# A convolution layer with neighbourhood attention: both transposes of the probabilities in one place

## The chip, the core and the metric

The kernel runs on one core of a Trainium2 chip. The metric is the device time of one execution in microseconds (us). Its engines work side by side and meet only at semaphores: TensorE (matrix products, in the rows PE, its weight loads PEld, its queue PEldq), VectorE (DVE), ScalarE (ACT), GpSimd (POOL, idle here after the start) and SyncE (SP), which issues the transfers.

## The reference, cut to what matters

Eight images of 128 x 128 pixels and 64 channels in fp32.

```python
stk = neighborhood(x)                       # 3x3 shifted views of x, zero padded
scores = einsum('bhwke,bhwe->bhwk', stk @ K_P, x @ Q_P) * mask
alpha = softmax(scores)                     # over the 9 neighbours
t_in = t = x + einsum('bhwk,bhwke->bhwe', alpha, stk @ V_P)
t = relu(conv3x3(t, ff1) + b1)              #  64 ->  64 channels
t = relu(conv3x3(t, ff2) + b2)              #  64 -> 128 channels
t = relu(conv3x3(t, ff3) + b3)              # 128 ->  64 channels
return t_in + t
```

## The kernel before, in words

The images are worked in 4 pairs, the 64 channels of one image on partitions 0 to 63 and of the other on 64 to 127. An image is cut into 16 bands of 8 rows. A pair takes 16 steps: k = 1 to 15, and k = 0 in which the last rows of one pair and the first of the next are worked together. Step G works the attention of band b = G + 1, the scores and softmax of band b + 2, the first convolution, and with one band's delay the second and third one. The names `k`, `b` and `att` in the code are these; `att == ASK` are the 60 steps in which a band of probabilities is still wanted. 53 of them run in a loop, which TensorE's code has for k = 2 to 15; k = 1 and k = 0 stand outside it, since their tiles leave rows out.

The three 3x3 convolutions use a one-dimensional Winograd form along the width: pairs of neighbouring columns are turned into four streams (`transform`, VectorE), four products are formed per pair, and sums and differences give the two output columns (`middle`, `outer`). Tile j of a convolution is one of the four streams. First and third convolution are fp32 products; a fp32 product shows as two half products in the trace. The second is taken from a high and a low part: `duh` (ScalarE, `u_high`) and `dul` (VectorE, `u_low`), times `w2h` and `w2l`. Its work on TensorE is 36 rounds, in each of which a product on the lower 64 rows of the array and one on the upper 64 run side by side: per tile j `begin2` (4 rounds), `go_on2` (2) and `end2` (3).

The attention of a band works on 16 patches of 8 x 8 pixels with their 10 x 10 = 100 keys. For a band, TensorE forms `r_product` and, masked, the `scores` (L426, L434); VectorE takes the maxima (`max_scores`, L932), ScalarE the exponentials with their sums (`exps`, L774), VectorE scales them (`scale`, L939 the reciprocal, L943 the multiplication, which raises `prob_ready`); TensorE transposes them (`turn`, L443: 16 transposes of 64 x 100 for each half of the band's patches, which raise `turned`), ScalarE copies them to SBUF (`keep_turned`, L791, raises `probt_ready`), and a step later TensorE mixes the keys with them (`mix`, L455) and forms the `v_product` (L465), to which VectorE adds x (`add_x`, L954). Half 0 of the scores lies in `far_banks`, half 1 in `near_banks`; the transposes of a half go to the same banks.

Each engine runs a program of its own, written out by hand for a step, and there is no planner. The parts that matter here:

- TensorE, `step` (L695 on): r_product, first convolution, v_product and scores between its parts, tiles 0, 1, 2 of the third convolution (`conv3_tile`, L514), the mixes, tile 3, then the second convolution with one half transposed ahead of `begin2(0)` and the other inside `go_on2(0)`. The waits for the second scaling stand in a function that `conv3_tile` and `go_on2` call in their middle (`ahead`): tile 3 has six taps, and it calls `ahead` before the last two (L525).
- `await_turn(b, half)` (L648) waits for `y_ready` (half 0 only) and for `prob_ready` of the half.
- VectorE, `step` (L1111 on), from add_x to the end: add_x, the inputs of the third convolution, the middle sums of the first, maxima 0, `outer1`, maxima 1, more inputs, middle sums of the third convolution (L1001, L1002), `scale(b + 2, 0)`, `u_low` 0 (L987), `scale(b + 2, 1)`, `outer3` (L1039, which waits for tile 3), `u_low` 1, `finish`, the inputs of the first convolution of the next step, middle sums of the second (L1005, L1006).
- ScalarE, `step` (L891 on): `keep_y` twice, `u_high` 1, `keep_turned` 0 and 1, then the copies of the second convolution.
- SyncE copies the last rows of `dodd` and `deven` to their front once tile 3 is done (L374 to L376); the next step's inputs wait for it.
- `begin2(0)` waits for the readers of the third convolution's banks 0 and 1 and for `duh`; `begin2(1)` for outer3 (L551); `begin2(2)` for `probt_ready` of both halves, because it overwrites their banks (L554).

Of the kernel before, what the change touches and what calls it, by code (L numbers as in the profile page):

```python
# [52 lines left out]
def bank_of(which, j):  # L53
    return j if which == CONV3 else 2 * j + (which == EVEN)


V, MIX, ASK = 1, 2, 3
# [10 lines left out]
def pairs3(k):  # L68
    return (0, 2) if k == LAST else (0, RP)
# [11 lines left out]
def build(nc, x_bands, x_keys, qt2, kt, vbd, w1, w2, w3, b1, b2, b3, window, eye, eye16, out):  # L81
    with ExitStack() as ctx:
# [6 lines left out]
        def sem(name):  # L89
            return ctx.enter_context(nc.semaphore(name))  # L90
# [98 lines left out]
        prob_ready = sem("prob_ready")  # L189
# [3 lines left out]
        y_ready = sem("y_ready")  # L193
# [47 lines left out]
        def middle_read(G, which, behind=0, image=1):  # L241
            n = {CONV1: 1 + image, CONV3: 4, ODD: 6, EVEN: 7}[which]
            return G * DVE_READS + (n + DVE_READS - DVE_READS * behind - (3 if G is FINAL else 0))

        def outer_read(G, which, behind=0):
            n = {CONV1: 3, CONV3: 5, ODD: 8, EVEN: 9}[which]
            return G * DVE_READS + (n + DVE_READS - DVE_READS * behind - (3 if G is FINAL else 0))
# [7 lines left out]
        def parts(G, part, behind=0):  # L255
            return G * 2 + (part + 1 + 2 - 2 * behind)
# [146 lines left out]
        def _(pe):  # L403
# [36 lines left out]
            def turn(b, half):  # L440
                for a in range(HALF):
                    for n, rows in enumerate((LOWER, UPPER)):
                        last = nc.tensor.transpose(score_banks[half][0:KEYS, n, a * C:(a + 1) * C],  # L443
                                                   prob[rows, 2 * half + a // GROUP, a % GROUP], eye_sb[rows, rows])
                        if a == HALF - 1:
                            last.then_inc(turned, 1)
# [49 lines left out]
            def conv3_tile(G, k, j, ahead=None):  # L496
                if j == 0:
                    pe.wait_ge(dve_read, middle_read(RUN, EVEN) if G is FINAL else middle_read(G, CONV1, image=0))
                elif j == 1 and G is not FINAL:
                    pe.wait_ge(dve_read, middle_read(G, CONV1))  # L500
                elif j == 2 and G is not FINAL:
                    pe.wait_ge(dve_read, outer_read(G, CONV1))
                lo, hi = pairs3(k)
                m, part = STREAMS[j], j // 2
                bank = conv_banks[:, bank_of(CONV3, j)]

                def tap(odd, s, start, stop):

                    rows, source = (LOWER, UPPER)[odd], (dodd, deven)[s % 2]
                    spans = [(lo, hi)]  # L510
                    if k == 1 and s in (0, 3):
                        spans = [(0, 2), (3, RP)] if s == 0 else [(0, 1), (2, RP)]
                    for lo_, hi_ in spans:
                        mm = nc.tensor.matmul(bank[rows, lo_ * 128:hi_ * 128], w3f[:, m, s, odd * C:odd * C + C],  # L514
                                              source[:, lo_ + s // 2:hi_ + s // 2, m], start=start,
                                              stop=stop and hi_ == hi)
                    return mm

                pe.wait_ge(d_done[ODD], parts(G, part, 1))
                tap(0, 2, True, False)  # L520
                tap(1, 2, True, False)
                tap(0, 0, False, False)
                pe.wait_ge(d_done[EVEN], parts(G, part, 1))
                tap(1, 1, False, False)
                if ahead:  # L525
                    ahead()
                tap(0, 1, False, True)
                tap(1, 3, False, True).then_inc(tile_done, 1)

            def tap2(k, which, j, rows, s, w, d, start, stop):  # L530

                lo, hi = pairs2(k)
                spans = [(lo, hi)]
                if k == 0 and (which, rows) == (EVEN, LOWER) and s == 0:
                    spans = [(0, 1), (2, RP)]
                if k == 0 and (which, rows) == (ODD, UPPER) and s == 1:
                    spans = [(1, RP)]
                for lo, hi in spans:
                    mm = nc.tensor.matmul(conv2_bank(which, j)[:, lo * 128:hi * 128],  # L539
                                          w[rows, STREAMS[j], 2 * (which == EVEN) + s],  # L540
                                          d[rows, lo + s:hi + s, STREAMS[j]], start=start, stop=stop)
                return mm
# [22 lines left out]
            def go_on2(G, k, j, ahead=None):  # L565

                pe.wait_ge(du_low, G * 2 + (j // 2 + 1))
                for s in range(2):
                    if ahead and s == 1:
                        ahead()  # L570
                    even = tap2(k, EVEN, j, LOWER, s, w2h, dul, False, False)
                    odd = tap2(k, ODD, j, UPPER, s, w2h, dul, False, False)
                even.then_inc(half_done, 1)
                odd.then_inc(half_done, 1)
# [66 lines left out]
            def await_v(G, b, att):  # L641
                if att:
                    pe.wait_ge(dve_read, outer_read(G, EVEN, 1))
                    pe.wait_ge(y_ready, b * 2 + 2)
                if att == ASK:
                    pe.wait_ge(r_ready, b * 2 + 6)

            def await_turn(b, half):  # L648
                if half == 0:
                    pe.wait_ge(y_ready, b * 2 + 4)  # L650
                pe.wait_ge(prob_ready, b * 2 + (half + 5))

            def values_and_scores(b, att):
                if att:
# [40 lines left out]
            def step(G, k, b, att):  # L695
                if att == ASK:
                    r_product(b + 2)
                if k in (0, DRAIN):
                    wholes(k, False, True, lambda: await_v(G, b, att))
                    quarters(k, False, False)  # L700
                    values_and_scores(b, att)
                    wholes(k, True, True)
                    quarters(k, True, False)
                else:
                    quarters(k, False, True)
                    if att:
                        pe.wait_ge(dve_read, outer_read(G, ODD, 1))
                        pe.wait_ge(y_ready, b * 2 + 2)
                        pe.sem_inc(phase_begun)
                        v_product(b)  # L710
                    if att == ASK:
                        pe.wait_ge(dve_read, outer_read(G, EVEN, 1))
                        pe.wait_ge(r_ready, b * 2 + 5)
                        pe.sem_inc(phase_begun)
                        masks(0)
                        scores(b + 2, 0)
                        pe.wait_ge(r_ready, b * 2 + 6)
                        pe.sem_inc(phase_begun)
                    quarters(k, True, True)
                    if att == ASK:  # L720
                        pe.wait_ge(t_ready, b + 1)
                        pe.sem_inc(phase_begun)
                        masks(1)
                        scores(b + 2, 1)
                    wholes(k, False, False)
                    wholes(k, True, False)
                conv3_tile(G, k, 0)
                conv3_tile(G, k, 1)
                conv3_tile(G, k, 2)
                if att >= MIX:  # L730
                    if att == ASK:
                        pe.wait_ge(exp_done, b * GROUPS + (2 * GROUPS + 2))
                    mix(b + 1, 0)
                    mix(b + 1, 1)
                conv3_tile(G, k, 3, (lambda: await_turn(b, 0)) if att == ASK else None)
                if att == ASK:
                    turn(b + 2, 0)
                begin2(G, k, 0, b, att)
                go_on2(G, k, 0, (lambda: await_turn(b, 1)) if att == ASK else None)
                if att == ASK:  # L740
                    turn(b + 2, 1)
                begin2(G, k, 1, b, att)
                go_on2(G, k, 1)
                end2(G, k, 0)
                end2(G, k, 1)
                begin2(G, k, 2, b, att)
                go_on2(G, k, 2)
                begin2(G, k, 3, b, att)
                go_on2(G, k, 3)
                end2(G, k, 2)  # L750
                end2(G, k, 3, lambda: await_next(G, b, att))
# [509 lines left out]
```

## Time and profile before

| | us |
|---|---|
| median of three runs (2067.3 to 2069.97) | 2067.95 |
| the profiled execution | 2069.45 |
| its span, first to last instruction | 2067.6 |
| TensorE busy (97% of the span) | 2014.8 |
| VectorE busy (88%) | 1817.8 |
| ScalarE busy (53%) | 1088.2 |

The profile is one execution. Busy time of matrix products is modelled at their ends, so it isn't the engine at its peak; the starts are what counts in the rows. The granted TensorE clock is 0.991 of full speed over the span. A row of the timeline gives the start, the time from there to the end, the engine, the line, what is written from what, shapes and a count; instructions that follow each other in one group are merged into one row, so the same instruction can stand in a longer or a shorter row, by the stretch that is asked for. In square brackets: the idle time before, and what ended it. All rows count from the start of the span.

### The profile page before, as it was taken

To read this page: it belongs to the slowest core of one execution; us is meant where nothing else is said; L and a number is where in the kernel's file an instruction comes from. 1 tells how busy PE (TensorE), PEld (TensorE's weight loads), DVE (VectorE), ACT (ScalarE), POOL (GpSimd) and SP (SyncE) were. 2 spreads that over 40 slices of the span, in tenths; PEclk is the share of its full clock that TensorE was granted. 3 is DMA by queue.
4 is the path that set the end of the run, shared out by engine and by line. 5 is a ranking of instruction groups with operands and counts; after the bars stand their busy time and mean duration, and the time that the engine had idled before them with its cause. 6 is when DMAs were issued, how large, how long until landed. Compare 5 with 4: busy or idle time off the path is not lost.

```text
span 2067.6 us, 61916 instructions
## 1 busy us (share of the span) xinstructions
PE 2014.8 (97%) x23818; PEld 1237.0 (60%) x23818; DVE 1817.8 (88%) x2502; ACT 1088.2 (53%) x3087; POOL 20.4 (1%) x28
## 2 busy tenths in 40 slices
PE   4799999999999999999999999999999999999998
PEld 3565665665665665665656665665666655655654
DVE  5699889989899889889889899899898899899886
ACT  4455455455455455455455455455455455455432
POOL 3000000000000000000000000000000000000000
PEclk8899999999999999999999999999999999999999
DMA  8455555554565554554555554554555554554542
GB/s 180 114 169 142 167 164 142 168 164 142 161 172 141 167 167 139 168 166 140 167 162 147 165 167 141 166 167 141 165 168 141 167 168 140 166 168 140 159 141 88
DMA packets 286054, 320.89 MB, mean 155 GB/s; under 512 B 87802, under 2 KB 220218, under 8 KB 279482
## 3 DMA queue, kind: packets, MB, share of 16 engines
q1 hardware_dynamic: 284814, 319.68, 53.9%
q8 instruction: 46, 0.75, 0.2%
q10 hardware_dynamic: 1168, 0.24, 0.1%
q14 instruction: 26, 0.21, 0.0%
HBM read 150.23 MB, written 33.82 MB: 89 GB/s over the span
## 4 chain that ended last, share of the span: by engine, by line
PE 96%; DVE 2%; ACT 1%; issue 1%; DMA 1%; ACTq 0%; DVEq 0%
PE conv_banks L514 32%; PE conv_banks L474 16%; PE conv_banks L539 13%; PE side_banks L539 13%; PE side_banks L455 6%; PE side_banks L434 4%; PE conv_banks L414 3%; PE side_banks L443 3%; PE side_banks L465 3%; PE side_banks L426 2%; DMA bias<-b 1%; PE conv_banks L455 0%; ACT prob L774 0%; DVE work L1048 0%; DVE prob L943 0%
## 5 line engine op out<-in xcount | busy, mean ns | idle before, releaser
L514 PE MATMUL conv_banks<-dodd,w3f 128*64 128x512 f32 (+1 forms) x1592 | 483.6, 580 | 6.4 <-DVE work L1015 4.7
L514 PE MATMUL conv_banks<-deven,w3f 128*64 128x512 f32 (+1 forms) x1592 | 483.5, 580 | 0.0
L774 ACT ACTIVATE prob<-side_banks,negmax 128x100 f32<-128x100 f32 x1024 | 345.2, 379 | 169.5 <-DVE negmax L932 169.5
L474 PE MATMUL conv_banks<-dt,w1f 128*64 128x256 f32 (+2 forms) x4128 | 378.4, 378 | 0.0
L474 PEld LDWEIGHTS conv_banks<-dt,w1f 128*64 128x64 f32 (+1 forms) x4128 | 233.9, 135 | 121.9 <-issue 43.0
L514 PEld LDWEIGHTS conv_banks<-dodd,w3f 128*64 128x64 f32 x1592 | 146.3, 137 | 236.5 <-issue 216.8
L774 ACT ACTIVATION_READ_ACCUMULATOR prob<-side_banks,negmax 128x1 f32 x1024 | 248.1, 242 | 0.0
L514 PEld LDWEIGHTS conv_banks<-deven,w3f 128*64 128x64 f32 x1592 | 150.5, 137 | 141.2 <-issue 137.8
L786 ACT COPY rq<-conv_banks 128x512 f32<-128x512 f32 x128 | 69.0, 592 | 299.7 <-PE conv_banks L414 299.7
L1048 DVE TENSOR_TENSOR work<-side_banks,work 128x1024 f32<-128x1024 f32 (+1 forms) x130 | 154.4, 1233 | 80.3 <-PE side_banks L539 80.3
L791 ACT COPY probt<-side_banks 100x1024 f32<-100x1024 f32 x128 | 129.9, 1017 | 155.5 <-PE side_banks L443 155.5
L539 PE MATMUL conv_banks<-duh,w2h 64*128 64x512 f32 (+2 forms) x788 | 167.4, 417 | 4.3 <-issue 3.7
L812 ACT COPY m_sb<-conv_banks 128x512 f32<-128x512 f32 x196 | 109.5, 593 | 100.8 <-PE conv_banks L539 97.0
L539 PE MATMUL side_banks<-duh,w2h 64*128 64x512 f32 (+2 forms) x788 | 158.1, 391 | 1.7 <-ACT probt L791 1.7
L987 DVE TENSOR_TENSOR dul<-work,duh 128x1024 fp32r<-128x1024 f32 (+1 forms) x130 | 156.7, 1205 | 2.8 <-ACT duh L841 2.8
L539 PE MATMUL side_banks<-duh,w2l 64*128 64x512 f32 (+2 forms) x788 | 156.7, 389 | 0.0
L539 PE MATMUL conv_banks<-duh,w2l 64*128 64x512 f32 (+2 forms) x788 | 156.1, 388 | 0.0
L833 ACT ACTIVATE relued<-work,bias 128x1024 f32<-128x1024 f32 (+1 forms) x130 | 142.2, 1145 | 23.2 <-DVE work L1048 23.2
L1039 DVE TENSOR_TENSOR work<-conv_banks,work 128x512 f32<-128x512 f32 x132 | 84.6, 682 | 71.7 <-PE conv_banks L514 71.4
L455 PEld LDWEIGHTS side_banks<-probt,xk 100*64 100x64 f32 x3968 | 127.0, 138 | 33.3 <-issue 32.1
L841 ACT CAST duh<-work 128x1024 fp32r<-128x1024 f32 (+1 forms) x130 | 139.3, 1072 | 3.9 <-DVE work L969 3.7
L932 DVE TENSOR_REDUCE negmax<-side_banks 128x8 f32<-128x800 f32 x128 | 125.4, 981 | 17.8 <-PE side_banks L434 17.8
(109 smaller groups left out, 3282.8 us busy)
## 6 DMA issues: line engine op xcount, KB each, us to landing
xk<-x_keys SPq DMA_DIRECT2D x64, 800.0 KB
xc<-x_bands SPq DMA_DIRECT2D x63, 650.0 KB, 4.9
xr<-x_bands SPq DMA_DIRECT2D x260, 128.0 KB, 2.9
dodd<-dodd SPq DMA_DIRECT2D x65, 512.0 KB, 5.7
out<-work SPq DMA_DIRECT2D x64, 512.0 KB, 4.2
dt<-dt SPq DMA_DIRECT2D x65, 256.0 KB, 4.9
deven<-deven SPq DMA_DIRECT2D x65, 256.0 KB, 6.2
duh<-duh SPq DMA_DIRECT2D x65, 256.0 KB, 2.3
```

The lines of the kernel that those rows point to most:

```text
L455: last = nc.tensor.matmul(banks[image, half, a * C:(a + 1) * C], xk[:, patch, image], probt[:, half, i if a < GROUP else 1 - i, a], start= ...
L474: mm = nc.tensor.matmul(bank[(LOWER, UPPER)[o], n * 256 + lo * 64:n * 256 + hi * 64], w1f[i][rows, m, s, o * C:o * C + C], dt[rows, lo + s ...
L514: mm = nc.tensor.matmul(bank[rows, lo_ * 128:hi_ * 128], w3f[:, m, s, odd * C:odd * C + C], source[:, lo_ + s // 2:hi_ + s // 2, m], start ...
L539: mm = nc.tensor.matmul(conv2_bank(which, j)[:, lo * 128:hi * 128], w[rows, STREAMS[j], 2 * (which == EVEN) + s], d[rows, lo + s:hi + s, S ...
L774: last = nc.scalar.activation(prob[:, g, a], score_banks[g // 2][:, g % 2, a * KEYS:(a + 1) * KEYS], ACT.Exp, bias=negmax[:, g, a:a + 1], ...
L791: nc.scalar.copy(probt[:, half], score_banks[half][0:KEYS].rearrange("n i (a q) -> n i a q", q=C)).then_inc(probt_ready, 1)
L812: nc.scalar.copy(m2_sb[:, which % 2, lo:hi], bank[:, lo:hi]).then_inc(act_read, 1)
L833: nc.scalar.activation(to[:, lo:hi, :, 1:1 + W], sums[which][:, lo:hi], ACT.Relu, bias=bias[:, 1:2]).then_inc(relu_done, 1)
L841: nc.scalar.copy(duh[:, 1:n + 1, streams], du[:, 0:n, streams]).then_inc(du_high, 1)
L932: nc.vector.tensor_reduce(negmax[:, 2 * half:2 * half + 2], score_banks[half][:, :, 0:GROUP * KEYS].rearrange("q g (a n) -> q g a n", n=KEYS),
L987: nc.vector.tensor_tensor(dul[:, 1:n + 1, streams], du[:, 0:n, streams], duh[:, 1:n + 1, streams].bitcast(F32), ALU.subtract).then_inc(du_ ...
L1048: nc.vector.tensor_tensor(both, m03, both, ALU.add).then_inc(dve_read, 1)
```

## The change

Both halves are waited for in tile 3 of the third convolution and transposed right behind it; the second convolution then runs from `begin2(0)` to the end of `end2(3)` without transposes in it. The steps outside `ASK` and the first step are as before, and so are the other engines.

```diff
-            def await_turn(b, half):
-                if half == 0:
-                    pe.wait_ge(y_ready, b * 2 + 4)
-                pe.wait_ge(prob_ready, b * 2 + (half + 5))
+            def await_turns(b):
+                pe.wait_ge(y_ready, b * 2 + 4)
+                pe.wait_ge(prob_ready, b * 2 + 6)
@@ step @@
-                conv3_tile(G, k, 3, (lambda: await_turn(b, 0)) if att == ASK else None)
-                if att == ASK:
-                    turn(b + 2, 0)
+                conv3_tile(G, k, 3, (lambda: await_turns(b)) if att == ASK else None)
+                if att == ASK:
+                    for half in range(2):
+                        turn(b + 2, half)
                 begin2(G, k, 0, b, att)
-                go_on2(G, k, 0, (lambda: await_turn(b, 1)) if att == ASK else None)
-                if att == ASK:
-                    turn(b + 2, 1)
+                go_on2(G, k, 0)
                 begin2(G, k, 1, b, att)
                 go_on2(G, k, 1)
```

## Rows read from the trace of the kernel before

**Rows 1.** The page, part 4: the chain that ended last, shares by engine.

```profile
PE 96%; DVE 2%; ACT 1%; issue 1%; DMA 1%; ACTq 0%; DVEq 0%
```

**Rows 2.** TensorE's waits, 120 to 1950 us: us in total, times, longest.

```profile
PE side_banks L426 <- DVE tf L954: 2.8, 3, 0.9
PE conv_banks L514 <- DVE work L1015: 1.1, 3, 0.4
```

**Rows 3.** Timeline of VectorE, a loop step.

```profile
995.45 1.29 DVE L954 TENSOR_TENSOR tf<-side_banks,xr 128x512 f32<-128x512 f32 x2 [0.66 <-PE side_banks L465]
...
1009.49 0.99 DVE L943 TENSOR_TENSOR prob<-prob,expinv 128x800 f32<-128x800 f32 x1
...
1011.76 0.99 DVE L943 TENSOR_TENSOR prob<-prob,expinv 128x800 f32<-128x800 f32 x1
```

**Rows 4.** Timeline of VectorE, end of that step and the next.

```profile
1021.47 0.68 DVE L1006 TENSOR_TENSOR work<-conv_banks,m_sb 128x512 f32<-128x512 f32 x1
...
1026.45 1.29 DVE L954 TENSOR_TENSOR tf<-side_banks,xr 128x512 f32<-128x512 f32 x2 [0.66 <-PE side_banks L465]
```

**Rows 5.** Timeline of TensorE, tile 3 to `begin2(1)` of that step.

```profile
1010.98 1.45 PE L514 MATMUL conv_banks<-dodd,w3f 128*64 128x512 f32 x5
...
1012.69 1.03 PE L514 MATMUL conv_banks<-deven,w3f 128*64 128x512 f32 x4
1013.65 0.65 PE L443 MATMUL side_banks<-eye_sb,prob 64*100 64x64 f32 x16
1014.12 0.48 PE L539 MATMUL conv_banks<-duh,w2h 64*128 64x512 f32 x2
1014.43 0.39 PE L539 MATMUL conv_banks<-duh,w2l 64*128 64x512 f32 x2
...
1015.13 0.63 PE L539 MATMUL conv_banks<-dul,w2h 64*128 64x512 f32 x4
1015.59 0.61 PE L443 MATMUL side_banks<-eye_sb,prob 64*100 64x64 f32 x16
1016.01 0.48 PE L539 MATMUL conv_banks<-duh,w2h 64*128 64x512 f32 x2
1016.33 0.39 PE L539 MATMUL conv_banks<-duh,w2l 64*128 64x512 f32 x2
```

**Rows 6.** TensorE's queue at L651 and L650: count, ns, first and last start (us).

```profile
L651 PEldq EVENT_SEMAPHORE  x60: 51/51/51, 111.6 to 1942.0; - x60
L651 PEldq EVENT_SEMAPHORE  x1: 51/51/51, 1010.7 to 1010.7; - x1
L650 PEldq ALU_OP  x53: 32/32/32, 141.8 to 1941.9; - x53
```

**Rows 7.** Timeline, two waits of TensorE on VectorE and their release.

```profile
562.62 1.29 DVE L954 TENSOR_TENSOR tf<-side_banks,xr 128x512 f32<-128x512 f32 x2 [2.72 <-PE side_banks L465]
564.06 0.36 PE L426 MATMUL side_banks<-window_sb,eye_sb 64*64 64x400 bf16 x4 [0.92 <-DVE tf L954]
567.71 0.41 DVE L1015 TENSOR_TENSOR work<-conv_banks,m_sb 128x256 f32<-128x256 f32 x1
568.17 1.08 PE L514 MATMUL conv_banks<-dodd,w3f 128*64 128x512 f32 x4 [0.37 <-DVE work L1015]
568.66 0.14 PEld L514 LDWEIGHTS conv_banks<-dodd,w3f 128*64 128x64 f32 x1 [0.29 <-issue]
```

**Rows 8.** Timeline of VectorE, behind tile 3 of the loop step.

```profile
1013.86 1.29 DVE L1039 TENSOR_TENSOR work<-conv_banks,work 128x512 f32<-128x512 f32 x2 [1.10 <-PE conv_banks L514]
```

**Rows 9.** Timeline, a step with k = 0.

```profile
578.92 0.99 DVE L943 TENSOR_TENSOR prob<-prob,expinv 128x800 f32<-128x800 f32 x1
579.53 0.60 PE L514 MATMUL conv_banks<-deven,w3f 128*64 128x512 f32 x2
```

**Rows 10.** Timeline, a step with k = 1.

```profile
609.57 0.99 DVE L943 TENSOR_TENSOR prob<-prob,expinv 128x800 f32<-128x800 f32 x1
609.64 0.59 PE L514 MATMUL conv_banks<-deven,w3f 128*64 128x512 f32 x1
```

## The prediction

> **What bounds the kernel now.** I read the page first. TensorE carries 96% of the chain that ended last [rows 1]: a microsecond that TensorE loses is a microsecond of the time. Then its waits in the steady part: 3.9 us in 1830, none of them on the probabilities [rows 2]. So the order on TensorE is fed almost perfectly, and the question is whether the new order is fed as well. The program asks for both halves of the probabilities before the last two taps of tile 3 of the third convolution; before, it asked for half 0 there and for half 1 five of 36 rounds into the second convolution, behind `begin2(0)` and the first round of `go_on2(0)`.
>
> So I put one steady step of VectorE beside the same step of TensorE. Its last pause ahead of the scalings is 0.66 us for TensorE's value product [rows 3]. From that product (add_x at 995.45) it runs without a pause to the end of the second scaling, 1011.76 + 0.99 = 1012.75. The step repeats after 31.00 us (add_x at 995.45 and 1026.45) [rows 3, 4]. The end of the second scaling is thus tied to TensorE's own value product; it won't come earlier because TensorE comes later.
>
> **The wait, in a steady step.** TensorE's tile 3 starts at 1010.98; each fp32 product shows as two half products and a pair of them takes 0.43 us. The last two taps start at 1012.69 and the transposes of half 0 at 1013.65 [rows 5]. The first scaling ends at 1009.49 + 0.99 = 1010.48, so the old wait costs nothing: TensorE's queue passes its event at 1010.7, far ahead of the taps it guards [rows 3, 6]. The new one needs 1012.75, 0.06 us after the two taps should start. To that comes the release. Bounds from two waits of TensorE on VectorE: at 563.91 (562.62 + 1.29) add_x ends and the product that waits for it starts at 564.06, so 0.15 us; at 567.71 + 0.41 = 568.12 a subtraction ends and the product starts at 568.17, 0.05 us, but its second half follows after 0.49 instead of 0.43 because the weights weren't loaded ahead, so 0.11 us in all [rows 7]. If both add up it is 0.21. The first of these waits is an event of its own in the queue, as ours is [rows 6], so I take 0.15. Stall: 1012.75 + 0.15 - 1012.69 = 0.21 us, ends 0.17 and 0.27. Behind the waiting instruction stand the two taps; behind them the transposes, VectorE's outer3, and SyncE's copies of dodd and deven; they all slide with TensorE. VectorE already waits 1.10 us for tile 3 [rows 8] and SyncE's copies are used a step later, so that delays nothing twice. But nothing gives the stall back either: from the transposes to the next value product TensorE has no slack, and VectorE's next scaling starts from that product. Each of the steady steps pays.
>
> **The two kinds of other step.** 60 steps transpose (the wait's event appears 60 times), 53 of them in the loop [rows 6]. Outside it are the 3 steps with k = 0 and the 4 with k = 1. With k = 0, the second scaling ends at 578.92 + 0.99 = 579.91 and the two taps start at 579.53: stall 579.91 + 0.15 - 579.53 = 0.53 [rows 9]. With k = 1, some taps leave rows out, so TensorE is at this point sooner: 609.57 + 0.99 = 610.56 against a tap at 609.64: stall 1.07 [rows 10].
>
> **What is gained.** The transposes themselves stay (32 in a step). Half 1 in the middle of the second convolution costs: round at 1015.13 with another one 0.23 later, rounds follow each 0.23, so the two next ones would be at 1015.60 and 1015.83; the second stands at 1016.33: 0.50 us. Appended to half 0 it adds eight pairs. The second half alone takes 1016.01 - 1015.59 = 0.42 up to the next round, the first, with its start, 1014.12 - 1013.65 = 0.47 [rows 5]. I take 0.45, so the gain is 0.05 us in a step, ends 0.03 and 0.08. What is saved is one hand-over from transposes back to rounds: the first round behind either half takes 0.31 (1014.12 to 1014.43) instead of 0.23.
>
> The Trainium skill (TensorEngine Tiling (Array Packing), Key Properties) says that changing the tiling mode drains the engine; this change takes two such changes out of each step. By that rule I would price both at what the third convolution pays before its transposes. The trace shows the way into the second half without a gap and so doesn't bear it out there; as a mechanism it is rival 2 below.
>
> **Edits at nothing.** The first round of `begin2(0)` comes 0.45 us later behind tile 3 and `begin2(1)` at the same place less 0.05. `begin2(1)` waits for outer3, which ends 1013.86 + 1.29 = 1015.15 [rows 8], 0.86 before its use at 1016.01. ScalarE's copy of half 1 has its input more than a microsecond earlier, and its reader, `begin2(2)`, stays where it was against the step. At the end of the step the wait for the last middle sum (1021.47 + 0.68 = 1022.15 [rows 4]) stands before the last third of `end2(3)`, which is over only when the next step begins: 0.05 less between them leaves cover. Were it gone, it would be bounded by the gain itself.
>
> **The sum.** Steady: 53 x (0.21 - 0.05) = 8.5. k = 0: 3 x (0.53 - 0.05) = 1.4. k = 1: 4 x (1.07 - 0.05) = 4.1. Together +14.0 us. The profiled execution took 2069.45 us (2067.6 span); so its like is 2083.5. The median of the three runs is 2067.95, 1.5 below the profiled one; the same 14 on it gives **2082 us**. Low end, stall 0.17 and gain 0.08: 53 x 0.09 + 3 x 0.41 + 4 x 0.95 = 9.8, so 2077.8. High end, 0.27 and 0.03: 53 x 0.24 + 3 x 0.56 + 4 x 1.10 = 18.8, so 2086.8.
>
> **Rivals.** (1) The wait is covered, and the time is not slower. This is one mechanism at one place: if the second scaling ends 0.21 us earlier against the taps, or if TensorE's queue already holds the two taps when it waits, only the gain is left, 60 x 0.05 = 3 us, 2065.0 (with 0.08, 2063.2). For it: the margin missed is only 0.06 us plus the release. Against it: VectorE's chain of 17 us has no pause to shrink, the wait stands in program order before the taps, and the queue did stop at such events [rows 7]. It decides at a stall of 0.05. Chance 0.12; a third of it over 4 us, as faster.
> (2) Removing the mid-run transposes saves two starts of the third convolution's kind. Before its transposes stands 1013.65 - 1012.69 = 0.96 us for two pairs of 0.43, a gap of 0.10 [rows 5]. Two of these are 0.20 instead of 0.05: 53 x 0.01 + 3 x 0.33 + 4 x 0.87 = 5.0, so 2073.0. Against it: the round at 1015.13 and its follower are over just as the second half starts at 1015.59. Chance 0.08, mostly still slower.
> (3) The stall drains the queue: TensorE's queue passes the event of this place 2.0 us ahead of the products that it guards (1010.7 and 1012.69), and after the stall it must fill again under a run of 32 short transposes and the register work before `begin2`. Price at most another 0.1 in 60 steps: 6 us, 2088. Against it: 0.86 us of taps follow the wait, in which it can fill. Chance 0.12.
> The forecast has the rest, 0.68.
>
> **Numbers.** Range for 8 in 10: 2072 (rival 2) to 2089 (rival 3). A measurement of this kernel can tell about 0.2%, 4 us. Slower by more: the forecast, rival 3 and most of 2, 0.86 less some for a gain that I undersized: 0.84. Same 0.12, faster 0.04.
>
> **What would show it.** After: TensorE's waits have a new line, conv_banks of the third convolution behind prob, some 60 times at 0.2, 0.5 (k = 0) and 1.1 us (k = 1), 16 to 18 us in all. The steady step takes 31.16 us instead of 31.00. The first rounds run at 0.23 each from `begin2(0)` to the end, and the transposes form one run of about 1.0 us. Wrong: a step of 30.95 (rival 1), waits as said but a step under 31.1 (rival 2), pauses among the transposes (rival 3).

## The result

The changed kernel takes 2086.09 us (median of 6 runs, 2084.69 to 2088.49) against 2069.59 (6 runs, 2067.3 to 2071.39): a ratio of 1.0083, with a 95% interval of 1.0070 to 1.0096, so 16.5 us slower. The forecast was 14 us more and a time of 2082. The profiled execution took 2087.91 us, its span is 2086.1.

The page of the changed kernel, parts 1 and 4, first line each:

```profile
PE 2025.2 (97%) x23818; PEld 1237.8 (59%) x23818; DVE 1816.7 (87%) x2502; ACT 1081.3 (52%) x3087; POOL 19.9 (1%) x28
...
PE 90%; DVE 5%; issue 2%; ACT 1%; DMA 1%; ACTq 0%; DVEq 0%
```

TensorE had 96% of the chain [rows 1] and has 90% now; VectorE's share rose from 2% to 5%, though TensorE's busy share is still 97%. The work is the same (23818 products), yet TensorE's busy time grew from 2014.8 to 2025.2 us. The next view shows why this is no contradiction. It is the timeline of a loop step of the changed kernel, first VectorE, then TensorE, to be read beside [rows 3, 5, 8]. Line numbers are two lower than before: L941 is the scaling, L952 add_x, L1037 outer3.

```profile
1002.03 1.29 DVE L952 TENSOR_TENSOR tf<-side_banks,xr 128x512 f32<-128x512 f32 x2 [0.68 <-PE side_banks L465]
...
1018.35 0.99 DVE L941 TENSOR_TENSOR prob<-prob,expinv 128x800 f32<-128x800 f32 x1
1020.69 1.29 DVE L1037 TENSOR_TENSOR work<-conv_banks,work 128x512 f32<-128x512 f32 x2 [1.35 <-PE conv_banks L514]
...
1033.26 1.29 DVE L952 TENSOR_TENSOR tf<-side_banks,xr 128x512 f32<-128x512 f32 x2 [0.70 <-PE side_banks L465]
```

```profile
1017.55 1.45 PE L514 MATMUL conv_banks<-dodd,w3f 128*64 128x512 f32 x5
1018.42 0.59 PE L514 MATMUL conv_banks<-deven,w3f 128*64 128x512 f32 x1
1018.85 0.59 PE L514 MATMUL conv_banks<-dodd,w3f 128*64 128x512 f32 x1
1018.85 1.71 PE L514 MATMUL conv_banks<-deven,w3f 128*64 128x512 f32 x5
1020.49 1.10 PE L443 MATMUL side_banks<-eye_sb,prob 64*100 64x64 f32 x32
1021.40 0.48 PE L539 MATMUL conv_banks<-duh,w2h 64*128 64x512 f32 x2
1021.72 0.39 PE L539 MATMUL conv_banks<-duh,w2l 64*128 64x512 f32 x2
1021.95 0.39 PE L539 MATMUL conv_banks<-duh,w2h 64*128 64x512 f32 x2
1022.18 0.40 PE L539 MATMUL conv_banks<-duh,w2l 64*128 64x512 f32 x2
1022.42 0.63 PE L539 MATMUL conv_banks<-dul,w2h 64*128 64x512 f32 x4
```

The row of five at 1018.85 spans the pause. The last two taps by themselves, from a shorter stretch:

```profile
1019.48 1.08 PE L514 MATMUL conv_banks<-deven,w3f 128*64 128x512 f32 x4
```

Same step, weight loads, and TensorE's queue at the wait:

```profile
1018.43 0.14 PEld L514 LDWEIGHTS conv_banks<-deven,w3f 128*64 128x64 f32 x1
...
1019.45 0.23 PEld L514 LDWEIGHTS conv_banks<-deven,w3f 128*64 128x64 f32 x4 [0.89 <-issue]
```

```profile
L650 PEldq EVENT_SEMAPHORE  x1: 51/51/51, 1019.4 to 1019.4; - x1
```

Tile 3 starts at 1017.55, so the transposes were due at 1017.55 + 2.67 = 1020.22 (before, 1013.65 - 1010.98 = 2.67 [rows 5]). They start at 1020.49: 0.27 late. The last two taps were due at 1017.55 + 1.71 = 1019.26 (before, 1012.69 - 1010.98 = 1.71) and the scaling ends at 1018.35 + 0.99 = 1019.34. The queue's event comes at 1019.4 instead of about 2 us ahead of the taps, the first of them starts at 1019.48, and the weights for the last taps are loaded only at 1019.45 instead of right behind those of the products before. Behind the transposes (now one run of 32, 0.91 us up to the first round) the first round takes 0.32 and the others follow each other at 0.23. The step takes 1033.26 - 1002.03 = 31.23 us instead of 31.00.

A wait in the middle of overlapping records is nearly invisible here. TensorE's waits from 120 to 1960 us; the first line is new against [rows 2]:

```profile
PE conv_banks L514 <- DVE prob L941: 3.1, 6, 0.7
PE side_banks L426 <- DVE tf L952: 2.8, 3, 0.9
PE conv_banks L514 <- DVE work L1013: 1.1, 3, 0.4
```

Only six pauses appear, those of the steps with k = 0 and k = 1 in this stretch (the first such step, at 111 us, is the seventh). A half product follows the other after 0.43 us but its record lasts 0.59, so the first 0.16 us of any pause count as busy. In 60 steps that is 9.6 of the 10.4 us more of busy time. It is the distance between starts that shows such a pause.

Where the 18.5 us between the two spans came from: up to add_x of the first step (96.40 and 94.24 us) the changed kernel was 2.16 ahead, a matter of start-up. From there to the last add_x of a step with transposes (1926.74 and 1942.71) it lost 18.13. The end took 2.53 more (140.86 and 143.39), 0.23 of it in one last step of the full length. The rest lies where TensorE's granted clock was lower: over the end, which has the same program in both, it is 0.95 of full speed instead of 0.98. The first 41 us behind the last add_x (from 1988.94 and 2005.15) take the same time in both, at a clock of 1.00; what follows takes 37.6 us before and 39.9 changed, at a clock of 0.94 and 0.86, with the same 232 products. The windows of the end, before and changed:

```profile
1955.00:2066.00 111.00, 102.08 (x828) 55.51 (x820) 87.65 (x132) 31.45 (x47) 0.00 (x0) 0.98 0.33 110
```

```profile
1971.00:2084.50 113.50, 104.56 (x832) 57.43 (x824) 87.86 (x132) 31.44 (x47) 0.00 (x0) 0.95 0.32 108
```

(The columns: PE, PEld, DVE, ACT, POOL busy, the clock as the third number from the end.) So the steps themselves carry 18.13 + 0.23 = 18.4 us, while the start took 2.2 us less and the end 2.3 us more. The median of six runs says 16.5; its interval is 14.5 to 19.9 us and holds both figures.

### The profile page after: what moved, and what is told of

It is laid out like the page before. It is cut to its first block, busy times and chain, and to the rows that moved or that the text cites. A ratio compares the mean times of both kernels' runs of the same rounds, so it can differ in the third digit from the quotient of the medians.

```text
span 2086.1 us, 61916 instructions
## 1 busy us (share of the span) xinstructions
PE 2025.2 (97%) x23818; PEld 1237.8 (59%) x23818; DVE 1816.7 (87%) x2502; ACT 1081.3 (52%) x3087; POOL 19.9 (1%) x28
## 4 chain that ended last, share of the span: by engine, by line
PE 90%; DVE 5%; issue 2%; ACT 1%; DMA 1%; ACTq 0%; DVEq 0%
PE conv_banks L514 30%; PE conv_banks L474 15%; PE conv_banks L539 13%; PE side_banks L539 13%; PE side_banks L455 5%; PE side_banks L434 4%; PE conv_banks L414 3%; PE side_banks L443 3%; PE side_banks L465 2%; PE side_banks L426 2%; DMA bias<-b 1%; DVE prob L941 1%; DVE work L1046 0%; DVE work L1021 0%; DVE negmax L930 0%
## 5 line engine op out<-in xcount | busy, mean ns | idle before, releaser
L514 PE MATMUL conv_banks<-deven,w3f 128*64 128x512 f32 (+1 forms) x1592 | 498.8, 584 | 6.9 <-DVE prob L941 3.8
L772 ACT ACTIVATION_READ_ACCUMULATOR prob<-side_banks,negmax 128x1 f32 x1024 | 243.5, 238 | 0.0
L789 ACT COPY probt<-side_banks 100x1024 f32<-100x1024 f32 x128 | 123.8, 1017 | 124.0 <-PE side_banks L443 124.0
L539 PE MATMUL conv_banks<-duh,w2h 64*128 64x512 f32 (+2 forms) x788 | 163.0, 405 | 4.3 <-issue 3.7
L1037 DVE TENSOR_TENSOR work<-conv_banks,work 128x512 f32<-128x512 f32 x132 | 84.6, 683 | 91.5 <-PE conv_banks L514 91.4
```

The source lines that it names most:

```text
L772: last = nc.scalar.activation(prob[:, g, a], score_banks[g // 2][:, g % 2, a * KEYS:(a + 1) * KEYS], ACT.Exp, bias=negmax[:, g, a:a + 1], ...
L789: nc.scalar.copy(probt[:, half], score_banks[half][0:KEYS].rearrange("n i (a q) -> n i a q", q=C)).then_inc(probt_ready, 1)
```

## Experiments

Runs of one kernel differ by 0.1 to 0.2% either way, which is as much as some of the effects below; the loop steps of one trace are nearly all within 0.03 us of each other. So each kernel is also judged by its loop step, taken as the distance of add_x over 12 steps of the second pair. Before: 31.00 us. Changed:

```profile
658.47 1.29 DVE L952 TENSOR_TENSOR tf<-side_banks,xr 128x512 f32<-128x512 f32 x2 [0.68 <-PE side_banks L465]
```

up to the 1033.26 above, 374.79 / 12 = 31.23.

**1. The wait alone.** The kernel before, half 1 still in the middle of the rounds, with both waits in tile 3.

```diff
-                if half == 0:
-                    pe.wait_ge(y_ready, b * 2 + 4)
-                pe.wait_ge(prob_ready, b * 2 + (half + 5))
+                pe.wait_ge(y_ready, b * 2 + 4)
+                pe.wait_ge(prob_ready, b * 2 + 6)
...
-                go_on2(G, k, 0, (lambda: await_turn(b, 1)) if att == ASK else None)
+                go_on2(G, k, 0)
```

> As the kernel before, with half 1 still transposed inside the second convolution, but both waits ahead of the last two taps of tile 3. Theory (wait): it pays the stalls of the changed kernel without its gain, so a loop step of 31.28 us and 19 to 22 us over the kernel before, 2 to 3 more than the changed one. Rival (the moved transposes cost the time): a loop step of 31.00 us and no difference from the kernel before.

Measured: 2086.35 us against 2068.75, ratio 1.0088 (1.0072 to 1.0103), 17.6 us. The step:

```profile
658.80 1.29 DVE L953 TENSOR_TENSOR tf<-side_banks,xr 128x512 f32<-128x512 f32 x2 [0.68 <-PE side_banks L465]
...
1033.96 1.29 DVE L953 TENSOR_TENSOR tf<-side_banks,xr 128x512 f32<-128x512 f32 x2 [0.67 <-PE side_banks L465]
```

375.16 / 12 = 31.26. The wait without the move costs all of it, and 0.03 a step more than the changed kernel, where 0.05 was expected; the time is a little under the expected 19 to 22. The 0.02 that are missing are in the changed kernel's stall: over its loop steps the transposes start 0.28 late (median), and 0.27 here. The move is not what costs.

**2. The move alone.** The changed kernel, both waits behind the tile.

```diff
-                conv3_tile(G, k, 3, (lambda: await_turns(b)) if att == ASK else None)
-                if att == ASK:
+                conv3_tile(G, k, 3)
+                if att == ASK:
+                    await_turns(b)
+                    pe.sem_inc(phase_begun)
                     for half in range(2):
```

(`phase_begun` is raised for nobody; it is the instruction that carries the wait.)

> As the changed kernel, but both waits stand behind the last tap of tile 3, ahead of the first transpose. Theory (the added time is the wait for the second scaling ahead of the two last taps): the scaling ends 0.9 us before the first transpose is due in a loop step, so nothing waits there; with k = 1 about 0.1 us is left. A loop step of 30.95 us, 2 to 3 us less than the kernel before, and 18 to 19 less than the changed one. Rival (a run of 32 transposes or a run of 36 rounds is slower than two runs, the wait is small): it stays at about 31.2 us in a loop step and 16 us over the kernel before.

Measured: 2065.99 us against 2068.75, ratio 0.9988 (0.9979 to 0.9997). The step:

```profile
651.20 1.29 DVE L954 TENSOR_TENSOR tf<-side_banks,xr 128x512 f32<-128x512 f32 x2 [0.68 <-PE side_banks L465]
...
1022.63 1.29 DVE L954 TENSOR_TENSOR tf<-side_banks,xr 128x512 f32<-128x512 f32 x2 [0.68 <-PE side_banks L465]
```

371.43 / 12 = 30.95: the predicted gain of 0.05 a step, 3 us in all, once the wait is covered.

**3. The scaling earlier.** The changed kernel, with VectorE's order changed and TensorE's left alone.

```diff
                     scale(b + 2, 0)
-                u_low(G, k, 0)
-                if att == ASK:
                     scale(b + 2, 1)
+                u_low(G, k, 0)
```

> As the changed kernel, but VectorE does the second scaling ahead of u_low 0 instead of behind it. Theory (wait): the scaling ends 1.1 us earlier, before the taps are due also with k = 1; the low part comes 1.2 us later and is ready at about the start of the transposes, before its rounds. A loop step of 30.95 us, 2 to 3 us less than the kernel before. Rival (the lateness moves on: the low part or ScalarE's exponentials become what TensorE waits for): a loop step of 31.1 or more, 6 us or more over the kernel before.

Measured: 2065.60 us, ratio 0.9984 (0.9975 to 0.9993).

```profile
651.26 1.29 DVE L952 TENSOR_TENSOR tf<-side_banks,xr 128x512 f32<-128x512 f32 x2 [0.67 <-PE side_banks L465]
...
1022.66 1.29 DVE L952 TENSOR_TENSOR tf<-side_banks,xr 128x512 f32<-128x512 f32 x2 [0.67 <-PE side_banks L465]
```

371.40 / 12 = 30.95 again. The second scaling, and tile 3 of the same step:

```profile
1007.00 0.99 DVE L941 TENSOR_TENSOR prob<-prob,expinv 128x800 f32<-128x800 f32 x1
1007.23 1.45 PE L514 MATMUL conv_banks<-dodd,w3f 128*64 128x512 f32 x5
```

It ends at 1007.99, 0.95 us before the last two taps are due (1007.23 + 1.71 = 1008.94). From the other side, the lateness of one VectorE instruction is the whole loss. These two are the fastest kernels of the study, 0.12% and 0.16% under the kernel before; they don't differ from each other by what can be measured.

**4. and 5. The scaling later, in both orders.** The reciprocals of the second scaling taken twice, once in the changed kernel, once in the kernel before.

```diff
-                nc.vector.reciprocal(expinv[:, groups], expsum[:, groups]).then_inc(inv_done, 1)
-                dve.wait_ge(inv_done, b * 2 + (half + 1))
+                for n in range(1 + half):
+                    nc.vector.reciprocal(expinv[:, groups], expsum[:, groups]).then_inc(inv_done, 1)
+                    dve.wait_ge(inv_done, b * 3 + (half + n + 1))
```

> As the changed kernel, but VectorE takes the reciprocals of the second scaling twice, with a wait between, so that the second scaling ends some 0.25 to 0.3 us later. Theory (the scaling is what TensorE waits for, and a stall recurs in each step with nothing giving it back): the whole delay in each of 60 steps, a loop step of about 31.5 us, and 31 to 35 us over the kernel before, 15 to 18 more than the changed one. Rival (the pauses of VectorE give part of it back): under 10 more than the changed one.

> The kernel before with the same doubled reciprocals. Theory (there the wait for half 1 has more than 2 us to spare): a loop step of 31.00 us, no difference. Rival (VectorE's length itself bounds the step): 0.25 us a step, 15 us over.

Measured in the changed kernel: 2098.76 us against 2068.72, ratio 1.0141 (1.0126 to 1.0157), 30 over the kernel before; in the kernel before: 2068.66, ratio 0.9998 (0.9988 to 1.0007). The changed kernel's rows: step, second scaling with its two reciprocals, and the wait.

```profile
663.54 1.29 DVE L953 TENSOR_TENSOR tf<-side_banks,xr 128x512 f32<-128x512 f32 x2 [0.68 <-PE side_banks L465]
...
1025.59 0.43 DVE L938 RECIPROCAL expinv<-expsum 128x8 f32<-128x8 f32 x2
1026.05 0.99 DVE L942 TENSOR_TENSOR prob<-prob,expinv 128x800 f32<-128x800 f32 x1
...
1040.96 1.29 DVE L953 TENSOR_TENSOR tf<-side_banks,xr 128x512 f32<-128x512 f32 x2 [0.65 <-PE side_banks L465]
```

```profile
PE conv_banks L514 <- DVE prob L942: 19.0, 58, 0.9
```

377.42 / 12 = 31.45 a step: 0.22 more than the changed kernel, and the pair of reciprocals takes 0.43 instead of 0.20. The delay came out a little smaller than the 0.25 to 0.3 assumed, hence 30 and not 31 to 35. All of it is paid in each step (0.22 of 0.23); VectorE's pauses gave nothing back. Now that the pauses are longer than the overlap of the records, the waits list them: 58 instead of 6. In the kernel before, the step stays at 31.00 (653.25 to 1025.25). So these 0.23 us of VectorE are free in the old order and paid one for one in the new.

**6. More hand-overs.** The kernel before, half 1 in four pieces, three of them behind rounds of `begin2(1)`.

```diff
-                    turn(b + 2, 1)
-                begin2(G, k, 1, b, att)
+                    turn(b + 2, 1, 0, 2)
+                begin2(G, k, 1, b, att, (lambda n: turn(b + 2, 1, 2 * n, 2 * n + 2)) if att == ASK else None)
@@ begin2, in the loop over s and w @@
+                        if piece and not (s == 1 and w is w2l):
+                            piece(1 + 2 * s + (w is w2l))
```

> As the kernel before, but half 1 is transposed in four pieces of four transposes, behind go_on2(0) and behind the first, second and third round of begin2(1). Three more runs of transposes inside the rounds. Theory (a run of transposes inside the rounds costs 0.05 us beyond its transposes, as one hand-over back): 3 x 0.05 in 60 steps, a loop step of 31.15 us and 8 to 10 us over the kernel before. Rival (each change of the tiling drains the array for 0.10 us, both ways): 3 x 0.20, a loop step of 31.60 us and 36 us over it.

Measured: 2078.64 us against 2068.72, ratio 1.0044 (1.0029 to 1.0060), 9.9 us. Timeline of TensorE there:

```profile
1018.45 0.63 PE L539 MATMUL conv_banks<-dul,w2h 64*128 64x512 f32 x4
1018.91 0.27 PE L443 MATMUL side_banks<-eye_sb,prob 64*100 64x64 f32 x4
1018.99 0.48 PE L539 MATMUL conv_banks<-duh,w2h 64*128 64x512 f32 x2
1019.31 0.28 PE L443 MATMUL side_banks<-eye_sb,prob 64*100 64x64 f32 x4
1019.39 0.48 PE L539 MATMUL conv_banks<-duh,w2l 64*128 64x512 f32 x2
```

The step is 31.17 (655.90 to 1029.94 over 12), 0.06 for each of the three added runs. The transposes start right behind the rounds (1018.45 + two rounds of 0.23 = 1018.91), and only the round behind them is long, 0.32. Three added runs of transposes cost 0.17 together; with 0.10 us at either end of each, as in rival 2, it would be 0.60. Rival 2 is out.

**7. Both runs in the middle.** The changed kernel with both waits in the middle of `go_on2(0)` and all transposes behind it.

```diff
-                conv3_tile(G, k, 3, (lambda: await_turns(b)) if att == ASK else None)
-                if att == ASK:
-                    for half in range(2):
-                        turn(b + 2, half)
+                conv3_tile(G, k, 3)
                 begin2(G, k, 0, b, att)
-                go_on2(G, k, 0)
+                go_on2(G, k, 0, (lambda: await_turns(b)) if att == ASK else None)
+                if att == ASK:
+                    for half in range(2):
+                        turn(b + 2, half)
```

> Both halves are transposed in one run inside the second convolution, where half 1 was before, and both waits stand there; none follows tile 3. Theory (wait): nothing waits, since the scaling is done 2 us earlier. If the 0.10 us ahead of the transposes behind tile 3 is the price of going from 128 to 64 rows, the second convolution pays it now, and a loop step takes 30.95 us, 2 to 3 us under the kernel before. If it is a price of transposes behind a fp32 product, it is gone: 30.85 us and 8 to 9 us under it. Rival (ScalarE's copies of the transposes come too late for begin2(2)): some tenths over 31.00 us.

Measured: 2068.45 us, ratio 0.9998 (0.9989 to 1.0007), a step of 31.02 (654.12 to 1026.34). None of the three expectations held. The rows:

```profile
1012.14 1.45 PE L514 MATMUL conv_banks<-deven,w3f 128*64 128x512 f32 x5
1013.52 0.51 PE L539 MATMUL conv_banks<-duh,w2h 64*128 64x512 f32 x2
1013.86 0.39 PE L539 MATMUL conv_banks<-duh,w2l 64*128 64x512 f32 x2
...
1014.56 0.63 PE L539 MATMUL conv_banks<-dul,w2h 64*128 64x512 f32 x4
1015.02 1.06 PE L443 MATMUL side_banks<-eye_sb,prob 64*100 64x64 f32 x32
1015.89 0.48 PE L539 MATMUL conv_banks<-duh,w2h 64*128 64x512 f32 x2
```

The second convolution now pays for coming behind fp32 products on 128 rows (0.10 us between 1012.14 + 3 x 0.43 = 1013.43 and 1013.52 by these rows, and a first round of 0.34 us), and again behind the transposes. Against experiment 2 that is one long first round more (0.34 instead of 0.23), and a run of 32 transposes that takes 0.87 instead of 0.91: 0.07, and the steps differ by 31.02 - 30.95 = 0.07. Call each start of a run of rounds, behind products of another form, an entry. This kernel has two of them, as the kernel before, and nearly the same time. Counting entries orders the results: one entry 30.95 (experiments 2 and 3), two entries 31.00 and 31.02 (before, 7), five entries 31.17 (6). This count was made after the results; no further run tested it. I had counted runs of transposes instead.

**8. and 9. The release.** The changed kernel, first with the two waits swapped, then with the wait for y moved behind the tile, so that the one for the probabilities stands alone.

```diff
-                pe.wait_ge(y_ready, b * 2 + 4)
                 pe.wait_ge(prob_ready, b * 2 + 6)
+                pe.wait_ge(y_ready, b * 2 + 4)
```

```diff
-                pe.wait_ge(y_ready, b * 2 + 4)
                 pe.wait_ge(prob_ready, b * 2 + 6)
@@ behind conv3_tile(G, k, 3, ...) @@
+                    pe.wait_ge(y_ready, b * 2 + 4)
+                    pe.sem_inc(phase_begun)
```

> As the changed kernel, but the wait for the probabilities is written ahead of the one for y, so that it sits on the weight load itself and the other one is the event in the queue. Theory (the release of an event of its own costs 0.15 us up to the product, on the weight load 0.05): each of the 60 stalls is 0.09 us shorter, a loop step of 31.14 instead of 31.23 us, 11 to 13 us over the kernel before. Rival (the release is the same wherever the wait sits): 31.23 us and 16 to 17 us over the kernel before.

> As the changed kernel, but only the wait for the probabilities stands ahead of the last two taps, alone, so that it can sit on the weight load; the wait for y follows the tile. Theory (of a stall, the release costs 0.15 us where the wait is a step of the queue, and 0.05 on the load): each of 60 stalls is 0.09 shorter, a loop step of 31.14 us and 11 to 13 us over the kernel before. Rival (release the same): 31.23 us and 16 to 18 us over it.

Swapped: 2082.43 us against 2068.75, ratio 1.0070 (1.0054 to 1.0085), a step of 31.20 (657.91 to 1032.32), so only 0.03 of the 0.09. The swap didn't do what it was made for: the load follows the scaling's end (1017.42 + 0.99 = 1018.41) by 0.13, and by 0.11 in the changed kernel (1019.34 to 1019.45):

```profile
1017.42 0.99 DVE L941 TENSOR_TENSOR prob<-prob,expinv 128x800 f32<-128x800 f32 x1
...
1018.54 0.20 PEld L514 LDWEIGHTS conv_banks<-deven,w3f 128*64 128x64 f32 x4 [0.91 <-issue]
```

```profile
L650 PEldq ALU_OP  x1: 32/32/32, 1018.5 to 1018.5; - x1
```

The trace's records name the semaphore that each instruction waits for. In both kernels the load carries the wait for y, and the wait for the probabilities is on the instruction ahead of it: the event at 1019.4 in the changed kernel, here a register step (the ALU_OP above) that belongs to the wait for y. The product follows the scaling's end by 0.13 instead of 0.15.

Alone: 2081.86 us against 2069.18, ratio 1.0059 (1.0046 to 1.0073), 12.7 us, a step of 31.13 (656.52 to 1030.06), 0.10 less than the changed kernel. The load follows the scaling (1015.24 + 0.99 = 1016.23) by 0.05:

```profile
1015.24 0.99 DVE L942 TENSOR_TENSOR prob<-prob,expinv 128x800 f32<-128x800 f32 x1
...
1016.28 0.20 PEld L514 LDWEIGHTS conv_banks<-deven,w3f 128*64 128x64 f32 x4 [0.84 <-DVE prob L942]
```

Here the wait for the probabilities is on the load. So the release, the time from the end of the scaling to what waited for it, was a real term of the sum, and 0.15 its size where the wait is an event of its own.

## Why the prediction was right

**The mechanism and the side: right.** The changed kernel waits where it was said to, for the second scaling ahead of the last two taps of tile 3, in each step, and nothing gives it back. Experiments 1 to 3 split the change into its two parts, +17.6 us and about -3 us; 4 and 5 show the one-for-one payment.

**The stall of a loop step: mis-sized.** Predicted was a stall of 0.21 less a gain of 0.05, a step of 31.16; it is 31.23. The release was taken as either 0.15, or 0.05 and 0.06 for weights not loaded ahead. Both come: the product starts some 0.15 us behind the scaling's end (1019.34 and 1019.48 above; with k = 0 below, 581.17 + 0.99 = 582.16 and 582.31; experiment 9 takes 0.10 of it away), and the late taps take some 0.05 us longer from their first half product to their last (0.49 instead of 0.44 in the changed kernel and in experiments 8 and 9 alike, as in [rows 7]). The late transposes give 0.27 in the step shown and 0.28 in the median, the high end that I had worked out and not taken. 53 x 0.07 is 3.7 us, most of the 4.4 between 14.0 and the 18.4 of the steps.

**k = 0 and k = 1: nearly right.** The steps with k = 1 were to cost 1.02 each: the first one is 31.28 instead of 30.22 us (94.24 to 125.52, before 96.40 to 126.62), 1.06, and the other three cost 0.99, 0.99 and 1.10. The three with k = 0 were to cost 0.48 and cost 0.56 each. For k = 0, the second scaling, and the taps before the pause and behind it, in the changed kernel:

```profile
581.17 0.99 DVE L941 TENSOR_TENSOR prob<-prob,expinv 128x800 f32<-128x800 f32 x1
```

```profile
581.36 0.59 PE L514 MATMUL conv_banks<-deven,w3f 128*64 128x512 f32 x1
582.31 1.08 PE L514 MATMUL conv_banks<-deven,w3f 128*64 128x512 f32 x4 [0.35 <-DVE prob L941]
```

0.95 instead of 0.43, so 0.52 where 0.53 was worked out, and 0.06 for the weights on top.

**The gain: right.** 0.05 a step by experiments 2 and 3. The kernels that have it make one entry less into the rounds.

**The edits at nothing: right.** `begin2(1)`, ScalarE's copies and the end of the step show no new wait.

**The rivals.** Rival 1 would have been true with the scaling some 0.3 us earlier or the wait behind the taps; experiment 2 put the wait there, experiment 3 brought the scaling forward by about 1 us, and both got its 3 us. Rival 2 fell with experiment 6. The rule of the Trainium skill (TensorEngine Tiling (Array Packing), Key Properties) that a change of the tiling mode drains the engine agrees with the 0.10 us between the third convolution's 128-row products and the 64-row ones behind them, transposes or rounds. Where rounds give way to transposes nothing is lost; but the rows have 64*128 for the one and 64*100 for the other, both 64 rows high, and no run shows whether this is a change of mode at all, as the prediction took it to be. So it says nothing against the rule. Rival 3, pauses among the transposes, doesn't show: 32 take 0.91 us up to the first round, the 0.47 of the first 16 [rows 5] and 0.44 more.

**What would show it: one point wrong.** I expected 16 to 18 us in the list of waits, some 60 times; it has 3.1, six times. The loss had to be read from starts.

**The number.** 2082 was forecast and 2086.09 measured, close under the high end of the sum, 2086.8. Of the 4 us between them 2.5 are the change itself; 1.6 are the base, since the three runs at hand had a median of 2067.95 and the six later ones 2069.59. That the medians differ by 16.5 and the steps carry 18.4 is within the interval; more about it wasn't tried.

## What to carry to other kernels

Put a wait right ahead of the instruction that needs it, and where an engine's queue forbids that, as late as it allows: here 0.9 us of taps that did not need the probabilities stood behind it, and moving the wait, not the work, turned +0.8% into -0.1%. Before merging two waits into the earlier place, find out when the later producer ends against that place. Here 0.06 us missed cost 0.27, because the release and the weights not loaded ahead are added to it, and it is paid in every step, because the producer's own start hangs on the waiting engine. And where the records of an engine overlap, read its pauses from the distance of starts.

## What the runs showed that I had not expected

The lists of waits named 7 of 60 pauses. In the loop step shown, the first late tap starts 0.22 us late (1019.48, due at 1019.26); 0.16 of it went into the overlap of the records and what was left was not listed. Of two waits in front of one instruction, the one for the probabilities stayed off that instruction in either order (load 0.11 and 0.13 us behind the scaling's end); standing alone it got onto it, with 0.05. And the way from 128-row fp32 products straight into the second convolution's rounds costs about as much as the way into them through the transposes (31.02 and 31.00 us a step), so that here the number of entries counted and not what lay between.
